# A state-space scan with float32 states, and with states in three passes of 16-bit halves placed behind the x projection

## The reference

```python
proj = hidden_states @ in_proj_w.T
gate, xBC, dt = split(proj)                      # xBC: causal convolution of 4 taps, then silu
dA  = dt * A;  cs = cumsum(dA, within a chunk of 128 tokens)
xdt = x * dt
scores = einsum('bclhn,bcshn->bchls', C, B) * where(tri, exp(cs_l - cs_s), 0)
Ydiag  = einsum('bchls,bcshp->bclhp', scores, xdt)
decay_states = exp(cs[..., -1:] - cs)
states = einsum('bclhn,bchl,bclhp->bchpn', B, decay_states, xdt)
prev   = scan over chunks: new = carry * exp(cs_last) + states    # carry is what a chunk sees
Yoff   = einsum('bclhn,bchpn,bchl->bclhp', C, prev, exp(cs))
y = Ydiag + Yoff + x * D
out = (y * silu(gate), normalised in each group of 1024) * norm_w @ out_proj_w.T
```

## Time and profile before

| | |
|---|---|
| median of 3 runs | 2519.56 us (2518.62 to 2520.28) |
| profiled execution: its time, its span | 2520.42 us, 2518.6 us |
| mean granted TensorE clock | 0.982 |
| TensorE busy | 2414.2 us (96%) |
| VectorE busy | 1822.8 us (72%) |
| ScalarE busy | 1588.6 us (63%) |
| GpSimd busy | 1246.3 us (49%) |

### The profile page before, as it was taken

How to read it: one execution, slowest core, us unless ns; L and a number is a source line. 1 busy time by engine, 2 the same in 40 slices (tenths; PEclk the granted TensorE clock), 3 DMA queues, 4 the chain that set the end, 5 groups by cost and what they waited for, 6 DMA issues and landing times. The chain is left out here.

```text
span 2518.6 us, 49367 instructions
## 1 busy us (share of the span) xinstructions
PE 2414.2 (96%) x15880; PEld 1387.2 (55%) x15880; DVE 1822.8 (72%) x3059; ACT 1588.6 (63%) x3318; POOL 1246.3 (49%) x986
## 2 busy tenths in 40 slices
PE   5999999999999999999999998789999999999797
PEld 3555555555555555555555554456566565655343
DVE  4777777777777777777777776577777777777433
ACT  5766766766766766766766775365656656566322
POOL 4456556556556455556556558333443343444123
PEclk8999999999999999999999999899999999999899
DMA  6333343243343343343343341320110110000000
GB/s 235 96 133 114 101 133 113 101 134 112 101 135 111 101 133 114 101 133 114 101 135 111 118 150 54 141 83 1 43 43 1 44 43 20 24 18 1 1 0 33
DMA packets 112867, 218.81 MB, mean 87 GB/s; under 512 B 9440, under 2 KB 42848, under 8 KB 110400
## 3 DMA queue, kind: packets, MB, share of 16 engines
q1 hardware_dynamic: 112576, 215.28, 26.1%
HBM read 212.10 MB, written 3.15 MB: 85 GB/s over the span
## 5 line engine op out<-in xcount | busy, mean ns | idle before, releaser
L1202 POOL TENSOR_TENSOR acc<-acc,sq 128x512 f32<-128x512 f32 x112 | 180.0, 1607 | 278.6 <-ACT sq L920 278.6
L908 ACT ACTIVATE E<-wq,cst 128x128 f32<-128x128 f32 x1024 | 311.6, 389 | 0.3 <-PEq L289 0.3
L255 DVE SCALAR_TENSOR_TENSOR xc<-bank,taps,xc 128x511 f32<-128x511 f32 (+2 forms) x384 | 284.3, 740 | 23.3 <-ACT xc L242 6.4
L1841 POOL TENSOR_TENSOR qT<-qT,qrot 128x512 f32<-128x512 f32 x64 | 81.2, 1268 | 376.4 <-DVE qrot L1743 376.4
L1188 POOL TENSOR_TENSOR ecs<-ecs,xcC 128x768 f32<-128x768 f32 x128 | 261.2, 2040 | 1.8 <-POOLq L289 1.8
L59 PE MATMUL bank<-xhi,wx 128*128 128x512 f16 x640 | 243.1, 380 | 2.9 <-DVE xcB L255 2.9
L1086 DVE SCALAR_TENSOR_TENSOR u<-xc,D,bank 128x512 f32<-128x512 f32 x128 | 95.7, 747 | 205.6 <-PE bank L737 191.6
L60 PE MATMUL bank<-xlo,wx 128*128 128x512 f16 x640 | 243.3, 380 | 0.0
L61 PE MATMUL bank<-xhi,wx 128*128 128x512 f16 x640 | 243.2, 380 | 0.0
L1025 DVE TENSOR_TENSOR E<-E,cbm 128x1024 f32<-128x1024 f32 x128 | 235.6, 1841 | 0.8
L920 ACT ACTIVATE sq<-u 128x512 f32<-128x512 f32 x112 | 70.2, 627 | 205.2 <-DVE u L1091 205.0
(11 more groups left out here) (243 smaller groups left out, 6464.3 us busy)
## 6 DMA issues: line engine op xcount, KB each, us to landing
wq<-cs_rows SPq DMA_DIRECT2D x128, 512.0 KB, 4.0
ecs<-ecs_rows SPq DMA_DIRECT2D x128, 384.0 KB, 3.6
wx<-in_w_xbc SPq DMA_DIRECT2D x80, 256.0 KB, 2.7
wz<-in_w_z SPq DMA_DIRECT2D x64, 256.0 KB, 2.7
wo<-in_w_o SPq DMA_DIRECT2D x64, 256.0 KB, 4.1
wq<-in_wq SPq DMA_DIRECT2D x8, 1024.0 KB, 5.7
awo<-in_wo SPq DMA_DIRECT2D x8, 1024.0 KB, 4.9
wkv<-in_wkv SPq DMA_DIRECT2D x8, 512.0 KB, 3.6
```

Source lines behind the costliest of these rows:

```text
L255: self.nc.vector.scalar_tensor_tensor(out=dst[:, d:T], in0=self.k.bank[bank][:, 0:T - d], scalar=self.taps[:, bass.ds(g, 1), b, j, 3 - d:4 ...
L908: ins = nc.scalar.activation(E[t.i % 4][:, h, c], sc.csr[t.i % 2][:, h, c * P:(c + 1) * P], ACT.Relu, scale=-1.0, bias=head(sc.cst, t, c, h))
L1202: nc.gpsimd.tensor_tensor(acc[t.b][:], acc[t.b][:], sq[:], ALU.add).then_inc(acc_done, 1)
```

## The change

The three float32 products of `states` become three passes of 16-bit halves each, by `product`, as the projections have them: nine matmuls of 128 columns. The halves are new:

- the transposed B: its copy on ScalarE writes `bthi` in float16 (one per unit, as before), and VectorE subtracts it from the bank into `btlo` (one per unit, slot 6);
- the decayed x: GpSimd writes `xw` as before, now into a single buffer, ScalarE copies it to `xwhi` in float16 at the head of the next slot, and GpSimd subtracts to `xwlo`, ahead of its decayed C. These two come once for each tile.

`wdec` is scaled up by 16 and the scale is taken out of the decayed C by a bias in its exponential in the setup. On TensorE `states(n1)` moves behind the projection of x, the gate comes right behind it and the transposes of x after the gate; the scan waits for the third state. On VectorE the masking of E moves ahead of the states, the states are spread over the remainder and the taps, and `xt` comes after the taps.

```diff
                 def states(t):
-                    pe.wait_ge(xw_done, t.n + 1)
-                    pe.wait_ge(bt_done, t.u + 1)
+                    pe.wait_ge(xwlo_done, t.n + 1)
+                    pe.wait_ge(btlo_done, t.u + 1)
+
+                    pe.wait_ge(xt_done, t.n + 1)
                     for c in range(CH - 1):
-                        mm = nc.tensor.matmul(W[:, c * P:(c + 1) * P], bt[t.b][:, c], xw[t.i % 2][:, c], start=True, stop=True)
+                        mm = product(nc, W[:, c * P:(c + 1) * P], (bthi[t.b][:, c], btlo[t.b][:, c]),
+                                     (xwhi[t.i % 2][:, c], xwlo[t.i % 2][:, c]), True, True)
...
                     scan(s)
-                    if tile_at(g, m + 1):
-                        states(tile_at(g, m + 1))
...
+                    if tile_at(g, m + 1):
+                        states(tile_at(g, m + 1))
+                        gate(tile_at(g, m + 1))
                     if tile_at(g, m + 2):
                         turn_x(g, m + 2)
-                    if tile_at(g, m + 1):
-                        gate(tile_at(g, m + 1))
...
+                def leading_x(t):
+                    act.wait_ge(xw_done, t.n + 1)
+
+                    wait(act, st_ready, t.n - 1)
+                    nc.scalar.copy(xwhi[t.i % 2][:], xw[:]).then_inc(xwhi_done, 1)
...
+                def rest_of_B(t, bank):
+                    dve.wait_ge(bt_done, t.u + 1)
+                    nc.vector.tensor_tensor(btlo[t.b][:], k.bank[bank][:, 0:(CH - 1) * P].rearrange("p (c n) -> p c n", n=P),
+                                            bthi[t.b][:], ALU.subtract).then_inc(btlo_done, 1)
...
-                    if n1:
-                        state(n1, 0)
                     dve.wait_ge(y_done, s.n + 1)
                     nc.vector.tensor_tensor(u[s.i % 2][:], u[s.i % 2][:], gz[s.i % 2][:], ALU.mult).then_inc(yg_done, 1)
                     if n1:
-                        state(n1, 1)
-                        state(n1, 2)
                         masked(n1)
                     if ended:
                         mean_square(s.u, s.b)
-                    if n2:
-                        turned_x(n2)
+                    if n1:
+                        state(n1, 0)
...
+                    remainder()
+                    if n1:
+                        state(n1, 1)
                     if n3:
-                        taps("x", sc.xc[n3.i % 4], n3, 2 + n3.i, (remainder, None))
-                    else:
-                        remainder()
+                        taps("x", sc.xc[n3.i % 4], n3, 2 + n3.i, (lambda: state(n1, 2), None))
+                    elif n1:
+                        state(n1, 2)
+                    if n2:
+                        turned_x(n2)
...
+                def rest_of_x(t):
+                    pool.wait_ge(xwhi_done, t.n + 1)
+                    nc.gpsimd.tensor_tensor(xwlo[t.i % 2][:], xw[:], xwhi[t.i % 2][:], ALU.subtract).then_inc(xwlo_done, 1)
...
                     if tile_at(g, m + 1):
+                        rest_of_x(tile_at(g, m + 1))
                         decayed_C(tile_at(g, m + 1))
```

More of the change, by code:

```diff
@@ L1 @@
+import math
 from collections import namedtuple
@@ L31 @@
 SPREAD = 4.0
+X_SCALE = 16.0
 def lead(words):
@@ L276, in setup @@
         cdT = k.sb("cdT", [P, TT], F32, tmp)
+        less = k.sb("less", [P, 1], F32, tmp)
         cdd = k.sb("cdd", [P, TT, P], F32, tmp)
@@ L376, in _ @@
                 act.wait_ge(v, 9)
-                nc.scalar.activation(ecsT[:], cs[:], ACT.Exp).then_inc(a, 1)
+                act.wait_ge(consts, 5)
+                nc.scalar.activation(ecsT[:], cs[:], ACT.Exp, bias=less[:]).then_inc(a, 1)
                 for c in range(TT):
@@ L387, in evacuate @@
                     act.wait_ge(tr, n + 1)
-                    nc.scalar.copy((sc.cst, sc.dtt, sc.wdec, sc.cd)[t][:, 4 * j:4 * j + 4].rearrange("p c g h -> p c (g h)"),
-                                   k.bank[4 + n % 4][:, :].rearrange("p (c h) -> p c h", h=P)).then_inc(ev, 1)
+                    nc.scalar.activation((sc.cst, sc.dtt, sc.wdec, sc.cd)[t][:, 4 * j:4 * j + 4].rearrange("p c g h -> p c (g h)"),
+                                         k.bank[4 + n % 4][:, :].rearrange("p (c h) -> p c h", h=P), ACT.Copy,
+                                         scale=X_SCALE if t == 2 else 1.0).then_inc(ev, 1)
                 act.wait_ge(loaded, 16 * 5)
@@ L405, in _ @@
                 nc.vector.memset(keep[:], 1.0).then_inc(consts, 1)
+                nc.vector.memset(less[:], -math.log(X_SCALE)).then_inc(consts, 1)
                 dve.wait_ge(consts, 3)
@@ L566, in mixer @@
         xt = [sb(f"xt{i}", [P, CH, P]) for i in range(2)]
-        xw = [sb(f"xw{i}", [P, CH - 1, P]) for i in range(2)]
+        xw = sb("xw", [P, CH - 1, P])
+        xwhi, xwlo = ([sb(f"xw{n}{i}", [P, CH - 1, P], F16) for i in range(2)] for n in ("hi", "lo"))
         st = [sb(f"st{i}", [P, CH - 1, P]) for i in range(2)]
@@ L575, in mixer @@
         cbm = [sb(f"cbm{i}", [P, CH, P]) for i in range(NB)]
-        bt = [sb(f"bt{i}", [P, CH - 1, P]) for i in range(NB)]
+        bthi, btlo = ([sb(f"bt{n}{i}", [P, CH - 1, P], F16) for i in range(NB)] for n in ("hi", "lo"))
         ms, rstd = sb("ms", [P, CH]), sb("rstd", [P, CH])
@@ L727, in scan @@
                     pe.wait_ge(cs_done, t.n + 1)
+                    pe.wait_ge(s_step, t.n * 3 + 3)
                     pe.wait_ge(gz_done, t.n + 1)
@@ L927, in gate @@
                     nc.scalar.activation(gz[t.i % 2][:], Y[:, :], ACT.Silu).then_inc(gz_done, 1)
+                def leading_x(t):
+                    act.wait_ge(xw_done, t.n + 1)
+                    wait(act, st_ready, t.n - 1)
+                    nc.scalar.copy(xwhi[t.i % 2][:], xw[:]).then_inc(xwhi_done, 1)
                 def turned_B(t, bank):
                     act.wait_ge(bt_ready, t.u + 1)
-                    nc.scalar.copy(bt[t.b][:], k.bank[bank][:, 0:(CH - 1) * P].rearrange("p (c n) -> p c n", n=P)).then_inc(bt_done, 1)
+                    nc.scalar.copy(bthi[t.b][:], k.bank[bank][:, 0:(CH - 1) * P].rearrange("p (c n) -> p c n", n=P)).then_inc(bt_done, 1)
                 def first():
@@ L942, in slot @@
                     s = tile_at(g, m)
+                    if tile_at(g, m + 1):
+                        leading_x(tile_at(g, m + 1))
                     if m % 2 == 0:
@@ L1123, in slot @@
                         masked_CB(nu, ring_bank(s.b, USE_CB))
+                    if nu and s.i == 6:
+                        rest_of_B(nu, ring_bank(s.b, USE_BT))
                     if ended:
@@ L1192, in decayed_x @@
                     pool.wait_ge(xt_done, t.n + 1)
-                    nc.gpsimd.tensor_tensor(by_head(xw[t.i % 2][:]), by_head(xt[t.i % 2][:, 0:CH - 1]), of_heads(sc.wdec, t, 0, CH - 1),
+                    wait(pool, xwlo_done, t.n)
+                    nc.gpsimd.tensor_tensor(by_head(xw[:]), by_head(xt[t.i % 2][:, 0:CH - 1]), of_heads(sc.wdec, t, 0, CH - 1),
                                             ALU.mult).then_inc(xw_done, 1)
+                def rest_of_x(t):
+                    pool.wait_ge(xwhi_done, t.n + 1)
+                    nc.gpsimd.tensor_tensor(xwlo[t.i % 2][:], xw[:], xwhi[t.i % 2][:], ALU.subtract).then_inc(xwlo_done, 1)
                 def accumulate(t):
@@ L1210, in first @@
                     decayed_x(tile_at(0, 0))
+                    rest_of_x(tile_at(0, 0))
                     decayed_x(tile_at(0, 1))
```

9 lines of the change are left out of this document (6 added, 3 removed).

## The result

2686.5 us median of 4 runs (2684.4 to 2690.3) against 2519.8 before: ratio 1.066, 95% interval 1.065 to 1.068. The forecast was 2698, in a range of 2575 to 2785. The profiled execution spans 2682.9 us, 164.3 more than before, and all of that lies in the state-space stage: the last `u` starts at 1731.89 instead of 1566.18.

The account below looks back on a forecast made before the run. VectorE's late third state, holding up TensorE's transposes of x, was taken to bound each slot: 0.15 + 0.8 x 1.55 = 1.39 us, times 128 = 178; 2520.4 + 178 - 0.9 = 2698 us, range 2575 to 2785.

Parts of the forecast that it names:

- The bound: TensorE's transposes of x wait until VectorE has taken the third state: +0.15 us a slot even without collisions.
- T: Start of the transposes of x, counted from the slot's `u`: 5.7 us in odd or 6.1 in even slots without collisions.
- T + 5.0: Slot period: from the start of the transposes to the next `u` it is 0.43 + 4.57 = 5.00 us.
- signs named: Transposes wait 150 to 230 us, nearly all slots; no `xwlo` wait; `u`*`gz`, `ylo` longer in most; E 2.1 or more.
- TensorE's saving: Nine 16-bit state matmuls cost 0.51 us instead of 0.78: 0.27 saved a slot, 35 in 128 slots.
- The collisions: VectorE's two-SBUF-input instructions and GpSimd's exclude each other for a whole instruction: +1.7 us a slot with every collision.
- 80% of 1.55: Share of collisions taken as met in each slot: 0.15 + 0.8 x 1.55 = 1.39 us.
- The sizes by sequence: With every collision: sequence 0 period 12.95 us, plus 2.2; sequence 1 period 11.95, plus 1.2.
- rival 4: More: every collision, about 0.9 us more in 32 slots after B or C, low clock possibly beyond: 2767 us; 14%.
- what follows the stage is untouched: Attention and what follows the state-space stage were taken as untouched by the change, adding nothing.
- rival 1: Transposes' wait is the bound, but engines settle with few collisions: +0.15 to +0.8 us a slot, 2539 to 2622; 18%.
- rival 2: Faster: VectorE gets the third state out before 5.46, TensorE's 35 us come through, 2485 us; 5%.

Follow-up runs that it names:

- run 1: Changed kernel with VectorE's second and third state right behind the first, ahead of the remainder `ylo` and the taps: 2583.9 us (ratio 1.026).
- run 2: Kernel before with only the change's new order on TensorE and VectorE; float32 states, no halves, copy or subtraction: 2575.0 us (1.022).
- run 7: Halves with the order of before; ScalarE's copy and GpSimd's subtraction brought forward into the slot in which `xt` is made: 2531.0 us (1.005).
- run 8: Run 7 with ScalarE's copy behind the gate's silu, and in slots 2 and 4 behind the B or C tap: 2502.6 us (0.993).
- run 9: Run 8 with GpSimd's split of `wz` behind the subtraction instead of ahead of the decayed x: 2498.8 us (0.992).
- run 4: Changed kernel with GpSimd's decayed C ahead of the new subtraction: 2592.0 us (1.028).
- run 3: Changed kernel with TensorE's and VectorE's order of before; halves, copy at the slot's head and subtraction stay: 2641.0 us (1.048).

## Why the prediction was right

**The bound.** Right. T is set by the third state in 104 of 127 slots (the wait's count), and T + 5.0 holds: 5.07 in the slot shown. In plain slots the medians are 5.06 to 5.08; slot 3 of sequence 1, with the low clock, has 6.75. Runs 1 and 2 show the bound from both sides. Of the signs named, the wait came in 104 slots but with 138.5 us in total, under the 150 to 230 that were said, and a wait for `xwlo` came that was ruled out; `u`*`gz` and `ylo` are longer in most slots, as said.

**TensorE's saving.** Right: 0.50 for nine passes against 0.78, and 0.24 to 0.26 a plain slot in runs 7 to 9, where nothing hides it.

**The collisions.** Right as a mechanism (run 4), with the order of events as predicted: copy, subtraction, `ecs` until +1.3 in the slot shown (+1.5 was said), `u`*`gz` held back by it. On `u`*`gz`, E and `ylo` together they add 1.7 us to a slot in the mean ((1.09 - 0.69) + (1.93 - 1.21) + (1.33 - 0.74)), more than the 1.24 that 80% of 1.55 makes, but not all of it moves T. E was expected at 2.1 or more; its mean is 1.93, and in plain slots it is often free while `ylo` is the one that collides. Without a collision `ylo` takes 0.74, close to the 0.6 plus its start that I used.

**The sizes by sequence.** Wrong. I had +2.2 a slot for sequence 0 and +1.2 for sequence 1. Measured are, in means, 105.2 against 95.1 us for the eight slots of sequence 0, which is +1.26 a slot, and 103.9 against 93.1 for sequence 1, which is +1.35. In sequence 0 the wait is 1.9 in odd slots (2.4 was said, as 7.9 less 5.46). In sequence 1 it is 0.54 in slot 1 and 1.06 in slot 7 (1.4 was said, as 6.9 less 5.46), but 2.2 and 2.1 behind B and C, where the transposes start at 7.85 and 7.74; every collision made 6.95 by the prediction. These are the 0.9 more that rival 4 gave to such slots, with subtraction and `ecs` both in VectorE's way. The low clock comes on top there, and the last unit.

**What the sum left out.** Two terms. The last unit: GpSimd prepares the weights of the linear layer there, the decayed x had a slot of room for that and the subtraction has none. In the trace:

```profile
1703.76 0.29 PE L62 MATMUL bank<-xwhi,bthi 128*128 128x128 f16 x1 [8.37 <-POOL xwlo L1230]
...
1722.79 0.29 PE L62 MATMUL bank<-xwhi,bthi 128*128 128x128 f16 x1 [7.04 <-POOL xwlo L1230]
```

These two and four shorter ones are 23.6 of the 28.3 us. I had written that what follows the stage is untouched and had not asked what stands ahead of the subtraction in the stage's own last slots. And the low clock, which the prediction had in rival 4 only. That the total came out within 12 us is in part luck. The last unit alone is 103.4 us from its first `u` to its last, 81.7 before, so 21.7 of the growth; over the other 120 slots the mean is 1.20 more than before, where 1.39 was said. A single share of 80% for all slots is not what the trace has. Read back from the start of the transposes, it fits the odd slots of sequence 0 (7.51, between 5.7 free and 7.95 with all), it is too much for slot 1 of sequence 1 (6.17, between 5.7 and 6.95) and far too much for its slots 2 and 4 (6.20 and 5.77, with 6.1 free), and too little behind B and C. The share was too high in the mean, and both missing terms are of the other sign. What bounds the kernel was right, and the size came out of errors that cancel.

**The rivals.** Few collisions (rival 1) is what run 4 makes of the kernel, 2592. Faster (rival 2) needed another place for the chain: runs 8 and 9.

**What the waits leave over.** Of the 165.7 us, 124.8 are the longer wait at the transposes and 23.6 that for `xwlo` in the last unit; the saving of 35 stands against them. By this account some 52 are missing. Most of them are found when the trace is read from start to start, because the modelled ends of matmuls make each idle time in front of the transposes look some 0.15 shorter than it is (609.33 - 608.42 - 0.22 = 0.69 for the 0.54 shown). So read, the wait at the transposes is longer by some 144, the output has 16.5 more at the low clock, the waits for `xwlo` are 24, the stretch from the output to the scan is 6 longer (the profile has 7.7 us of waits there at the loop's end and names no releaser), and the states with the start of what follows them are 33 shorter. Some 8 us stay open.

## What to carry to other kernels

A bank that two steps share ties their order on every engine: before a producer is moved behind cover, count what stands ahead of its consumer's last read on the engine that empties it. A helper instruction can cost more by where it pushes its neighbours in the queue than by its own time: here the place of one 1.8 us instruction was worth 94 us, because of what it collided with. And a collision costs only where somebody waits for what stands behind it: in run 9 E is nearly as long as in the changed kernel (1858 and 1931 ns), and the time is 188 us less. If splitting an operand saves TensorE time, bring the whole chain of helpers into the slot in which the operand is made, and look at the last tiles, where other work shares the queue.

## What the runs showed of the hardware

In 11 slots of the changed kernel the output ran in part at the low clock, granted 0.50, behind a single wait of 2.1 to 2.5 us (nine) or 1.90 us (two) on an otherwise full TensorE; seven waits of 2.1 to 2.2 us and nearly all of 1.9 had no such sequel. I had not expected it from one gap of that size. In run 3 the same came behind waits for `xwlo`, and the x projection paid for it. A float32 product of 128x128x128 took 0.26 (0.78 / 3), three 16-bit passes of it 0.17 (0.50 / 3). `u`, a VectorE instruction with one of its two large inputs in PSUM, took 0.74 to 0.75 us in all 128 slots of the changed kernel, in 117 of which GpSimd was at work beside it.
